# A conditioned GRU on one Trainium2 core: a different engine loop structure and a different order of the loads ahead of it

## The reference

```python
vz, vr, vh = video @ C_z + b_z, video @ C_r + b_r, video @ C + b     # video: (32, 512)
xz, xr, xh = seq @ W_z, seq @ W_r, seq @ W                           # seq = x, all steps
def step(h, xs):
    z = sigmoid(xzt + h @ U_z + vz)
    r = sigmoid(xrt + h @ U_r + vr)
    hh = tanh(xht + (r * h) @ U + vh)
    h_new = (1 - z) * h + z * hh
    return h_new, h_new
return x + states
```

## Time and profile before

| | |
|---|---|
| time, median of 3 runs | 2264.65 us (2261.95 to 2265.0) |
| profiled execution, own time | 2264.97 us |
| its span | 2263.1 us |
| PE, PEld, DVE, ACT, POOL busy | 97%, 79%, 78%, 59%, 30% of the span |
| HBM read, written | 43.25 MB, 33.55 MB |

### The profile page before, as it was taken

How to read it: one execution, slowest core, us unless ns; L and a number is a source line. 1 busy time by engine, 2 the same in 40 slices (tenths; PEclk the granted TensorE clock), 3 DMA queues, 4 the chain that set the end, 5 groups by cost and what they waited for, 6 DMA issues and landing times.

```text
span 2263.1 us, 238050 instructions
## 1 busy us (share of the span) xinstructions
PE 2185.4 (97%) x107502; PEld 1797.5 (79%) x107502; DVE 1754.5 (78%) x8226; ACT 1326.6 (59%) x4623; POOL 687.8 (30%) x1546
## 2 busy tenths in 40 slices
PE   2899999999999999999999999999999999999996
PEld 1788878888888887888888888788878888888875
DVE  5687878778778777777777777777777877877874
ACT  3566556566566665666656666556656656656652
POOL 0233333333333333333333333333333333333331
PEclk9999999999999999999999999999999999999998
DMA  9110110110110110111101101101101101101101
GB/s 196 34 38 19 38 38 19 38 37 19 38 33 23 38 35 22 38 29 28 38 24 33 38 24 32 38 19 37 38 19 38 38 19 38 38 20 38 28 11 22
DMA packets 145390, 78.48 MB, mean 35 GB/s; under 512 B 9024, under 2 KB 140608, under 8 KB 145216
## 3 DMA queue, kind: packets, MB, share of 16 engines
q1 hardware_dynamic: 145216, 76.84, 14.1%
HBM read 43.25 MB, written 33.55 MB: 34 GB/s over the span
## 4 chain that ended last, share of the span: by engine, by line
PE 95%; issue 2%; SPq 1%; DMA 1%; DVE 0%; ACT 0%; DVEq 0%; POOLq 0%; POOL 0%
PE p_bank L269 44%; PE c_bank L259 20%; PE banks L297 16%; PE banks L306 15%; SPq L152 1%; DMA x_nat<-in_x_dram 1%; SPq L147 0%; SPq L163 0%; PE p_bank L278 0%; DVE taken L631 0%; DVE state L635 0%; DVE h_t L639 0%; ACT gate_c L430 0%; SPq L155 0%; DVE h_lo L597 0%
## 5 line engine op out<-in xcount | busy, mean ns | idle before, releaser
L269 PE MATMUL p_bank<-w_hi,x_t 128*32 128x384 f16 x16384 | 1183.1, 327 | 2.4 <-issue 1.6
L269 PE MATMUL p_bank<-w_lo,x_t 128*32 128x384 f16 x8192 | 701.7, 327 | 2.2 <-issue 2.2
L269 PEld LDWEIGHTS p_bank<-w_hi,x_t 128*32 128x32 f16 x16384 | 462.3, 97 | 155.2 <-issue 1.5
L259 PEld LDWEIGHTS c_bank<-u,reset_t 128*32 128x32 f32 x32704 | 488.4, 110 | 98.6 <-DVE reset_t L611 71.7
L259 PE MATMUL c_bank<-u,reset_t 128*32 128x64 f32 x32704 | 551.0, 219 | 8.4 <-issue 8.1
L230 POOL TENSOR_TENSOR result<-x_nat,state 128x128 f32<-128x128 f32 x512 | 233.9, 457 | 1010.0 <-DVE h_lo L597 1008.4
L423 ACT ACTIVATE gate_r<-banks,gates_down 128x64 f32<-128x64 f32 x1024 | 265.6, 310 | 359.1 <-PE banks L297 358.1
L430 ACT ACTIVATE gate_c<-c_bank 128x64 f32<-128x64 f32 x1024 | 228.3, 223 | 302.8 <-PE c_bank L259 302.6
L216 POOL TENSOR_TENSOR kept<-keep,state 128x128 f32<-128x128 f32 x512 | 235.7, 460 | 551.3 <-ACT keep L426 551.3
L609 DVE TENSOR_TENSOR reset<-gate_r,state 128x64 f32<-128x64 f32 x1024 | 209.0, 204 | 209.3 <-ACT gate_r L423 205.8
L419 ACT ACTIVATE h_hi<-h_t 128x64 f16<-128x64 f32 x1024 | 261.0, 255 | 148.0 <-DVE h_t L639 80.4
(11 more groups left out here) (68 smaller groups left out, 2749.6 us busy)
## 6 DMA issues: line engine op xcount, KB each, us to landing
x_nat<-in_x_dram SPq DMA_DIRECT2D x256, 128.0 KB, 3.1
out_dram<-result SPq DMA_DIRECT2D x256, 128.0 KB, 2.8
w_stage<-in_L_cond_W_r_dram SPq DMA_DIRECT2D x4, 256.0 KB, 5.4
w_stage<-in_L_cond_W_z_dram SPq DMA_DIRECT2D x4, 256.0 KB, 8.1
w_stage<-in_L_cond_W_dram SPq DMA_DIRECT2D x4, 256.0 KB, 10.8
u<-in_L_cond_U_z_dram SPq DMA_DIRECT2D x4, 256.0 KB, 13.5
u<-in_L_cond_U_r_dram SPq DMA_DIRECT2D x4, 256.0 KB, 16.0
c_w<-in_L_cond_C_r_dram SPq DMA_DIRECT2D x4, 256.0 KB, 12.7
```

Source lines behind the costliest of these rows:

```text
L259: last = nc.tensor.matmul(c_bank[part(j), a, 0:N // HALVES], reset_t[:, part(q)], u[:, C, q, half_cols(j, a)], start=False, stop=q == Q - ...
L269: last = nc.tensor.matmul(p_bank[k][part(j), 0:G * N], x_t[:, c, part(q), a], w[b][:, :, q, cols(j)], start=f == 0, stop=f == GROUPS - 1, ...
```

## The change

Five things change together.

- PE's steps 1 to 512 become 128 rounds of one loop with a body of 4 steps, with a hint, its head at a fixed slot of a fetch block (slot 0). Step 512 does not exist in the problem. Its products run on what lies in the buffers and nobody reads them. The last two real steps now have their `project` too. ACT and DVE raise the semaphores that these extra pieces wait for.
- DVE's step is cut in two: `begin` (`h_lo`, `seed_c`, the head of x's scaling) and `go_on` (everything from `reset` on). The loop's body is now `go_on(tt)`, `begin(tt + 1)`, so the jump back lies between `seed_c` and `reset`. Its head is at slot 8.
- `load_weights` makes one DMA for each row quarter q: 128 partitions, one row of 2 KB for each, the source seen as 4 blocks j of 32 rows. `cond_nat` and each bias become one DMA, where the DRAM side has the block index j outermost as well.
- The order of the loads is W_r, W_z, x block 0, W_h, cond, U_z, U_r, biases, C_r, C_z, C_h, U_h, x blocks 1 to 3, and the wait for U_h between them is gone. The preamble's steps on PE, ACT and DVE are in another order, and the two gate bases are made by one instruction.
- The last block is stored in two parts: seven steps once `out_ready` reaches 511, and the last step in one DMA for all four blocks.

```diff
-    SPLITS = (R, Z, C, UZ, UR)
+    SPLITS = (R, Z, C, UR, UZ)
+    PE_SLOT, DVE_SLOT = 0, 8
...
             def load_weights(tile, source, done):
-                rows = source.rearrange("(j q s) e -> j s q e", j=J, q=Q)
-                for p in range(J):
-                    sp.dma_start(tile[part(p)], rows[p]).then_inc(done, 16)
-
-            for p in range(J):
-                sp.dma_start(cond_nat[part(p)], cond[:, cols(p)]).then_inc(s_cond_in, 16)
+                rows = source.rearrange("(j q s) e -> q j s e", j=J, q=Q)
+                for q in range(Q):
+                    sp.dma_start(tile[:, q], rows[q]).then_inc(done, 16)
+
+            load_weights(w_stage[:, R], W_r, s_w_in[R])
+            load_weights(w_stage[:, Z], W_z, s_w_in[Z])
             load_x(0, 0)
-            for g, m in enumerate((W_r, W_z, W_h)):
-                load_weights(w_stage[:, g], m, s_w_in[g])
+            load_weights(w_stage[:, C], W_h, s_w_in[C])
+            sp.dma_start(cond_nat[:], cond.rearrange("b (j e) -> j b e", j=J)).then_inc(s_cond_in, 16)
             load_weights(u[:, Z], U_z, s_u_in[Z])
             load_weights(u[:, R], U_r, s_u_in[R])
             for g, b in enumerate((b_r, b_z, b_h)):
-                for p in range(J):
-                    sp.dma_start(bias[part(p), g], b[cols(p)].unsqueeze(0).to_broadcast([B, N])).then_inc(s_bias_in, 16)
+                sp.dma_start(bias[:, g], b.rearrange("(j e) -> j e", j=J).unsqueeze(1).to_broadcast([J, B, N])).then_inc(s_bias_in, 16)
             for g, c in enumerate((C_r, C_z, C_h)):
                 load_weights(c_w[:, g], c, s_c_in[g])
-            load_x(1, 1)
             load_weights(u[:, C], U_h, s_u_in[C])
-            sp.wait_ge(s_u_in[C], 16 * J)
-            for n in range(2, BUFS):
+            for n in range(1, BUFS):
                 load_x(n, n)
...
+                if last and j == BODY - 1:
+                    sp.wait_ge(out_ready, T - 1)
+                    for p in range(J):
+                        sp.dma_start(out_rows[n, p][:, 0:BLOCK - 1], result[j % OUTS][part(p), 0:BLOCK - 1])\
+                            .then_inc(result_out[j % OUTS], 16)
+                    sp.wait_ge(out_ready, T)
+                    sp.dma_start(out_rows[n][:, :, BLOCK - 1], result[j % OUTS][:, BLOCK - 1]).then_inc(result_out[j % OUTS], 16)
+                    return
...
+            pe.wait_ge(x_t_ready, 3)
             total_x(TOTAL_STEP % 2, 0, 0, 3)
-            pe.wait_ge(x_t_ready, 3)
             project(0, 2, 0, GROUPS)
-            def step(m, tt, last, candidate_in=None):
...
+            pe.wait_ge(s_w_hi, len(SPLITS))
+            pe.wait_ge(s_w_lo, len(SPLITS))
+            pe.wait_ge(s_u_in[C], 16 * Q)
...
-            step(0, 1, True, s_u_in[C])
-            with pe.Fori(0, SETS - 3) as m:
-                for tt in range(2, SET + 2):
-                    step(m, tt, False)
-            for s in range(SET * (SETS - 3) + 2, T):
-                step(s // SET, s % SET, True)
+            with nc.Fori(0, SETS, engines=[pe.engine], hint_back_edge=True, head_slot={pe.engine: PE_SLOT}) as m:
+                for tt in range(1, SET + 1):
+                    step(m, tt)
...
+                if last and tt == STEPS - 1:
+                    dve.sem_inc(seeded, 1)
+                    dve.sem_inc(c_seeded, 1)
+                    dve.sem_inc(h_lo_ready, HALVES)
+                    dve.sem_inc(reset_t_ready, HALVES)
                 renew(1)
                 turn(1)
 
-            with nc.Fori(0, PASSES - 1, engines=[dve.engine], hint_back_edge=True) as i:
+            begin(0, 0, True)
+            rest_of_w(4)
+            with nc.Fori(0, PASSES - 1, engines=[dve.engine], hint_back_edge=True, head_slot={dve.engine: DVE_SLOT}) as i:
                 for tt in range(STEPS):
-                    step(i, tt, False)
+                    go_on(i, tt, False)
+                    begin(i, tt + 1, False)
```

More of the change, by code:

```diff
@@ L280, in total, with clear_bits @@
                 return last
-            def clear_bits(tile):
-                for g in range(2):
-                    nc.tensor.matmul(tile[:, g], zeros[:, 0:P], zeros[:], start=True, stop=True).then_inc(s_bits, 1)
+            def clear_bits(cells):
+                nc.tensor.matmul(cells, zeros[:, 0:P], zeros[:, 0:N], start=True, stop=True).then_inc(s_bits, 1)
             def total_x(k, c, of, sets):
@@ L312, in _ @@
                 total_x(1, m, 1 + m, m + 1)
[L313 to L319, removed]
+            pe.wait_ge(s_w_up, W_C + 1)
+            total_w(U_GATES)
+            pe.wait_ge(s_cond_t, 1)
+            for g in range(G):
+                pe.wait_ge(s_c_in[g], 16 * Q)
+                product(base_cell(g), cond_t, c_w[:, g], first=True).then_inc(s_base_mm, 1)
+            pe.wait_ge(s_w_up, U_GATES + 1)
+            pe.wait_ge(s_zeros, 1)
+            for g in range(GATES):
+                clear_bits(cell(0, g))
+            clear_bits(c_bank[:, 1, 0:N])
             pe.wait_ge(s_w_hi, G)
@@ L324, in _, with step @@
                 project(s, s, 0, GROUPS)
[L325 to L333, removed]
             pe.wait_ge(seeded, 1)
-            pe.wait_ge(c_seeded, 1)
             pe.sem_inc(r_mm, 1)
             pe.sem_inc(z_mm, 1)
+            pe.wait_ge(c_seeded, 1)
             pe.sem_inc(c_mm, HALVES)
+            pe.wait_ge(x_t_ready, 3)
             total_x(TOTAL_STEP % 2, 0, 0, 3)
-            pe.wait_ge(x_t_ready, 3)
             project(0, 2, 0, GROUPS)
-            def step(m, tt, last, candidate_in=None):
+            pe.wait_ge(s_w_hi, len(SPLITS))
+            pe.wait_ge(s_w_lo, len(SPLITS))
+            pe.wait_ge(s_u_in[C], 16 * Q)
+            def step(m, tt):
                 s = m * SET + tt
                 c, k = tt % SET, tt % 2
[L346 to L352, removed]
+                now = pe.snap(s + 1)
+                halves = [pe.snap(HALVES * s + (a + 1)) for a in range(HALVES)]
                 pe.wait_ge(seeded, now)
@@ L439, in step @@
                 now_m = i * (STEPS // SET) + m
+                if first and tt == 0:
+                    act.wait_ge(x_in[1], 16 * J)
+                    act.wait_ge(x_summed, 2)
+                    sum_x(2, 0)
+                if t == SUM_STEP and not more(3):
+                    act.sem_inc(x_summed, 1)
                 if t == SUM_STEP and more(3):
@@ L578, in _, with begin @@
             seed_gates(0, 0)
-            dve.wait_ge(s_bits, 6)
-            def step(i, tt, last):
+            dve.wait_ge(s_bits, GATES + 1)
+            def begin(i, tt, last):
                 s = i * STEPS + tt
@@ L604, in step, with go_on, count, more @@
                     scale_down((m + 1) % 2)
+            def go_on(i, tt, last):
+                s = i * STEPS + tt
+                m, t = divmod(tt, SET)
+                now_m = i * (STEPS // SET) + m
+                old, new = state[:, (tt - 1) % SLOTS], state[:, tt % SLOTS]
+                def count(v):
+                    return v if last else dve.snap(v)
+                now = count(s + 1)
+                def more(sets):
+                    return not (last and m + sets >= STEPS // SET)
                 for a in range(HALVES):
@@ L622, in step @@
                 dve.wait_ge(kept_ready, now)
-                if not (last and tt >= STEPS - TURN_AHEAD):
+                if last and tt >= STEPS - TURN_AHEAD:
+                    dve.sem_inc(x_t_ready, 1)
+                else:
                     ahead_m, c = divmod(tt + TURN_AHEAD, SET)
```

99 lines of the change are left out of this document (51 added, 48 removed).

## The result

| | before | after |
|---|---|---|
| time, median | 2264.31 us (4 runs, 2261.95 to 2265.0) | 2290.19 us (4 runs, 2289.34 to 2291.26) |
| profiled execution, own time | 2264.97 us | 2291.26 us |
| its span | 2263.1 us | 2289.4 us |
| ratio to before, 95% interval | | 1.0116 [1.0099, 1.0134] |

The change makes the kernel slower by 1.2%. The forecast was 2305 us with a range of 2284 to 2364.

A forecast was written before the change was run, and what follows sets the result against it. DMA bandwidth was taken to bound the start, PE the middle and PE's instruction supply the end. Sum: 2265.0 + 69.2 + 1.1 - 1.4 - 9.6 - 18.9 = 2305.4 us, range 2284 to 2364.

The forecast's parts named there:

- 4. x block 1 lands later: Preamble loads: weight DMAs on four of 16 engines, 12.0 us a weight, x block 1 at 119.0 us, +69.2 us.
- from there to the first product: PE's loop entry at a fixed slot: a jump to a block perhaps not there, between 0 and 1.6, taken as +1.1 us.
- 1. DVE's jump back: DVE's loop: the jump moved behind `seed_c` is hidden by the wait for `gate_r`, so all 9.6 us go.
- 2. PE's written-out end: PE from step 502 on: looping replaces straight code fetched by DMA, 47.0 us instead of 65.9, so 18.9 us go.
- 3. PE's first round: PE's first loop round: four steps instead of five have to be fetched, so 1.4 us go.
- The new order costs and gains nothing: Preamble: reordered products, bases, projections, scales and splits all lie inside the loading, so 0 us.
- the split store gains nothing: Kernel's end: PE's extra step ends last, by about 1 us, so storing the last block in two parts gains nothing.
- A: Rival on the loads: all 16 engines still carry each DMA, faster, 2227 to 2236, say 2232 us; chance 0.12.
- B: Rival on the loads: four engines at the crowd's 14.2 GB/s each, 18.5 us a weight, 2364 us; chance 0.10.
- C: Rival on the loops: DVE's jump still costs 1.6 us and PE's hint shows, 2312 to 2320 us; chance 0.07.
- D: Rival on PE's loop: its seven fetch blocks are refetched each round, 128 us in all, 2433 us; chance 0.03.
- fast bound: Loads at the quickest engine rate, 9.8 us a weight: +49.4 us on x block 1, 2285.6 us in all.

The follow-up runs named there:

- experiment 4: The kernel before with only PE's loop of 128 rounds at slot 0 and the semaphore increments it needs: 2247.5 us, ratio 0.9901.
- experiment 5: The kernel before with only the two new loops, PE's 128 rounds at slot 0 and DVE's rotated loop at slot 8: 2235.39 us, ratio 0.9868.
- experiment 1: The whole changed kernel, but weights loaded by 32-partition blocks as in the kernel before: 2243.44 us, ratio 0.9894 to the kernel before.
- experiments 6 to 8: Experiment 1 with DVE's loop not rotated, at slot 8 (2249.31 us) and slot 0 (2257.86 us); experiment 5 with DVE's loop at slot 0 (2238.71 us).
- experiment 3: The changed kernel with each quarter's weight DMA split into two of 64 partitions, outermost dimension 2: 2381.62 us, measured once.
- experiments 5 and 9: The second of these is experiment 5 without a fixed slot for DVE's loop: 2239.17 us, ratio 0.9888 to the kernel before.

## Why the prediction was right

The sign, the range and the two opposed terms were right. The errors of the terms do not cancel, they mostly add up, to 14.1 us. By its steps, in microseconds:

| step | predicted | measured | from |
|---|---|---|---|
| 4. x block 1 lands later | +69.2 | +59.2 | chain: 109.03 against 49.79 |
| from there to the first product | +1.1 | -1.1 | 5.04 against 6.19 |
| 1. DVE's jump back | -9.6 | -12.8 | 2152.08 - 2164.84 |
| 2. PE's written-out end | -18.9 | -18.4 | 2164.84 - 2178.97 - 4.23 |
| 3. PE's first round | -1.4 | -0.6 | 6.4 against 7.0 |
| sum | +40.4 | +26.3 | spans |

The 2178.97, 2164.84 and 2152.08 us are the times from PE's first `ALU_OP` of the loop to the end of the span, in before, experiment 4 and after:

```profile
L371 PEldq ALU_OP  x125: 32/32/32, 84.1 to 2195.9; - x125
...
L364 PEldq ALU_OP  x128: 32/32/32, 80.8 to 2243.9; - x128
```

Experiment 4 and after differ in DVE's loop there, before and experiment 4 in PE's end; before's first round holds one step more, hence the 4.23.

*The loads: the mechanism was right, the size too large by 10.* Two lines of PE's timeline give the distance between weights:

```profile
72.70 1.94 PE L254 MATMUL banks<-c_w,cond_t 128*32 128x128 f32 x32 [10.27 <-DMA c_w<-in_L_cond_C_r_dram]
83.31 1.93 PE L254 MATMUL banks<-c_w,cond_t 128*32 128x128 f32 x32 [8.67 <-DMA c_w<-in_L_cond_C_z_dram]
```

It is 10.6 us, and 10.7 to the next, where I took 12.0 between the bounds 9.8 and 13.7. The mis-sized term is 9 x (12.0 - 10.65) = 12.2 us too much, and the small loads (x blocks, cond, biases) took 2.2 more than the 9.0 I gave them: 2.0 + 9 x 10.65 + 11.2 = 109.0. The row of an engine with the queue to itself, 26.7 GB/s, was nearly the rate (24.6). Midway to the 19.2 GB/s of a thinned crowd was too cautious, and that row should not have been used at all. It counts the 17 packets of 0.1 us, and the stretches just before and behind it read

```profile
30.60:30.70 0.10, 0.00 (x0) 0.00 (x0) 0.10 (x1) 0.00 (x0) 0.00 (x0) 1.00 1.05 205
...
30.80:30.90 0.10, 0.00 (x0) 0.00 (x0) 0.10 (x1) 0.00 (x0) 0.00 (x0) 1.00 1.16 287
```

The same division makes 12.2 and 15.5 GB/s of them, so 19.2 was scatter and no sign of a faster engine. C_h's product began at 94.0, one weight and the x block ahead, and covered its followers, as the text said with 105.

*"The new order costs and gains nothing" holds only under slow loads.* I named the cover, the loading, but no price if it is gone. Experiment 5 against experiment 1 gives it: 7.4 us, for the new order of the loads and of the preamble together. The same goes for DVE's entry into its loop at slot 8, which I had not charged at all. After shows it too:

```profile
100.39 2.34 DVE L536 SCALAR_TENSOR_TENSOR uz_lo<-u,w_up,uz_hi 128x2048 f16<-128x2048 f32 x1
106.52 0.23 DVE L627 TENSOR_TENSOR reset<-gate_r,state 128x64 f32<-128x64 f32 x1 [3.79 <-issue]
```

DVE is through with step 0 at 109.03, in the moment in which x block 1 arrives, so none of this shows in the time. The charge for PE's own entry, +1.1, did not come either: PE's sequencer jumped at 111.8, inside the projection, the first product followed with no idle time, and even the 1.60 us of "issue" of the earlier trace rows are down to 0.14.

*DVE's jump: the size was too small.* I took the sum of PE's waits for `h_lo`, 9.6 us in seven waits. Only six of them lie at jumps back. Set against after step by step, experiment 4 loses 1.65 us in each step with a jump, 9.9 us, and 0.9 at 1998 us, in DVE's written-out steps 30 us behind the loop, where the kernel before has the same stall. That is 10.8. The other 2 us of the 12.8 are spread over all steps, and where they come from stays open. The waits show less than a stall costs:

```profile
876.43 0.29 PE L297 MATMUL banks<-ur_lo,h_hi 128*32 128x128 f16 x8
878.15 0.29 PE L297 MATMUL banks<-ur_hi,h_lo 128*32 128x128 f16 x8 [1.43 <-DVE h_lo L597]
```

These two groups of the kernel before start 1.72 us apart, the first of them 0.11 after the group ahead of it, so 1.61 us are lost where the wait says 1.43: it counts only from the modelled end of the group before. The text took the jump as cheap because ACT's was. That was the right value on a reason that isn't the right one: the first table of experiments 6 to 8 shows that a jump without cost needed the slot and the rotation together, and with one alone 0.6 or 0.9 us a round would have stayed.

*PE's end and first round.* PE's first round took 137.4 - 114.1 = 23.3 us, 6.4 more than four steps of 4.233; the text had 7.0 - 1.4 for these and called them fetching. "Four steps instead of five have to be fetched, so 1.4 us go" is not borne out: experiment 4 spent 7.4 us there and experiment 5 spent 5.6, so what this round takes more does not go by the number of steps alone. The end itself came out at 18.4 where 18.9 was foretold. The end, in start us, us, instruction:

```profile
2284.78 0.46 POOL L236 TENSOR_TENSOR result<-x_nat,state 128x128 f32<-128x128 f32 x1 [1.76 <-DVE state L655]
2285.26 0.64 SPq L178 DMA_DIRECT2D out_dram<-result  x1
2288.81 0.34 PE L275 MATMUL p_bank<-w_hi,x_t 128*32 128x384 f16 x4
```

PE ends last, at 2289.15, 3.9 us after the last store's issue began, and the split store gains nothing, as foretold. Experiment 5, which kept the four stores, ends on PE as well.

*The rivals.* A falls by the share of 0.28. B falls by 24.6 GB/s an engine, not 14.2. C falls by PE's 500.00 of 500. D falls by PE's 16.93 us a round. The time lies nearer the fast bound of 2285.6 than the forecast, as the lone engine's row would have had it. The step that weighed most, dealing out by the common outer dimension, was taken on a rule and not on a row; experiment 3 is the run that makes it this kernel's own.

## What to carry to other kernels

Ahead of a DMA's size and number, look at the outermost dimension that both its sides share: with 32 the DMA share here was that of 16 engines, with 4 that of 4. A cover that hides a cost ("it lies inside the loading") needs its own price beside it, because the next change may take the cover away; here 7.4 us lay under slow loads. And take a stall's cost from the period of the loop or from the starts of the steps, not from the waits that carry its name.

## What the runs showed of the hardware that was not expected

- By the DMA shares, one engine moves 24.6 to 25.5 GB/s when 2 or 4 of them work and 12.6 to 15.4 when all 16 do (202 to 247 GB/s). What holds the sixteen back isn't shown: each of their DMAs wrote into 32 partitions, those of the four into 128 and those of the two into 64, and no run has 16 engines with one DMA for 128 partitions.
- The total of the 32-partition loads is not one number. In before's order 10 to 30 us gave 223 GB/s from one queue and 247 from two, in after's order 216 and 215. The Trainium skill, "SBUF — State Buffer", "Door 1: The DMA port swizzle", gives an estimate of 217 GB/s for 32 partitions, near the 216 and 223 of one queue. Why two queues brought more in one order and not in the other no run shows.
- Splitting each quarter's load in two, with outermost dimension 2 instead of 4, halved the rate: 102 to 51 GB/s.
- After a jump back DVE went on some 1.76 us after an 8 KB packet of q14 had started, or some 0.55 us after the jump, whichever was later. A fixed slot 8 instead of 0 started that packet 0.6 to 2.8 us sooner.
- Entering a loop whose head is at slot 8 left DVE idle for 2.9 us, against 0.43 without a slot. Against slot 0 that slot made 64 steps 0.5 or 0.9 us shorter. Even so slot 8 was 4.5 us faster by the spans than no slot (experiments 5 and 9).
- PE's jump back cost nothing that the period shows, in 125 or 128 rounds, with a hint and a slot or without.
